# A graph network's source stage: rows landed one per descriptor, three of eight source tiles filled by accumulating gathers

## The reference, cut to what matters

```python
h = relu(layernorm(x));  x = x + attention_layer(h, edges)      # first layer
h = relu(layernorm(x))                                          # second layer:
msg = concat([h[row], h[col], edge_attr])                       # row = src, col = dst
t   = relu(msg @ W1 + b1) @ W2 + b2
x   = x + segment_sum(t, row, n)                                # sums over the SOURCE node
```

## Time and profile before

| | us |
|---|---|
| median of three runs | 5703.44 |
| the profiled execution | 5709.14 |
| its span, first to last instruction | 5707.3 |
| TensorE busy | 5097.3 (89%) |
| weight loads busy | 4028.8 (71%) |
| VectorE busy | 3955.6 (69%) |
| GpSimd busy | 3878.4 (68%) |
| ScalarE busy | 2972.5 (52%) |
| source stage, first load to last gather | 4364.8 to 5668.9 |

### The profile page before, as it was taken

One profiled execution on the slowest core, in us unless ns is written; L12 is line 12 of the kernel. 1 busy time (PEld: TensorE's weight loads), 2 busy tenths in 40 slices (PEclk: granted clock), 3 DMA queues, 4 the chain that ended last, 5 costly groups with the idle time before them and its releaser, 6 DMA issues.

```text
span 5707.3 us, 159502 instructions
## 1 busy us (share of the span) xinstructions
PE 5097.3 (89%) x33692; PEld 4028.8 (71%) x33693; DVE 3955.6 (69%) x14408; ACT 2972.5 (52%) x8485; POOL 3878.4 (68%) x3713
## 2 busy tenths in 40 slices
PE   4888888888888885999999999999997999999999
PEld 3677777767777774677666666666665787777877
DVE  6778878878887886455555555555545888888887
ACT  3566666666666653333333333333223777777776
POOL 4777777777777774677777777777776555555553
PEclk6888888898888887999999999999998999999999
DMA  4522222222222234999999899998886999999997
GB/s 109 163 53 54 52 53 54 53 53 53 53 54 53 54 105 135 268 271 268 263 261 261 255 265 264 260 260 260 258 256 191 216 221 219 215 217 218 220 218 191
DMA packets 859992, 990.85 MB, mean 174 GB/s; under 512 B 307993, under 2 KB 663225, under 8 KB 859776
## 3 DMA queue, kind: packets, MB, share of 16 engines
q1 hardware_dynamic: 662496, 608.23, 41.0%
q0 software_dynamic: 190592, 378.22, 24.7%
q10 hardware_dynamic: 6816, 3.38, 0.2%
HBM read 726.65 MB, written 262.76 MB: 173 GB/s over the span
## 4 chain that ended last, share of the span: by engine, by line
PE 56%; DMA 11%; issue 11%; POOL 9%; DVE 8%; DVEq 3%; ACT 2%; POOLq 0%; ACTq 0%; SPq 0%
PE bank L1705 12%; PE bank L1538 10%; PE bank L1628 9%; PE bank L1630 7%; PE bank L1695 7%; DMA xr<-arena 6%; POOL xr L547 5%; POOL arena L499 4%; PE bank L1464 2%; DMA arena<-h_tab,arena 2%; DVE arena L1055 2%; DVE arena L945 2%; PE bank L1618 2%; DMA arena<-p_tab,arena 1%; PE bank L1686 1%
## 5 line engine op out<-in xcount | busy, mean ns | idle before, releaser
L499 POOL DMA_INDIRECT arena<-h_tab,arena x1612 | 1564.3, 970 | 549.2 <-issue 407.6
L547 POOL DMA_INDIRECT xr<-arena x1612 | 1569.6, 974 | 515.4 <-issue 341.6
L1538 PE MATMUL bank<-arena 128*128 128x136 f32 x6448 | 1314.0, 332 | 72.7 <-DVE arena L1055 8.4
L719 ACT ACTIVATE arena<-bank 128x256 f32<-128x256 f32 x1612 | 593.5, 385 | 1393.6 <-PE bank L1630 944.5
L1628 PE MATMUL bank<-arena 128*128 128x256 f32 x3224 | 1031.4, 402 | 82.6 <-DVE arena L1251 44.1
L561 POOL DMA_INDIRECT arena<-p_tab,arena x428 | 669.7, 1565 | 630.9 <-DMA arena<-p_tab,arena 527.0
L1538 PEld LDWEIGHTS bank<-arena 128*128 128x128 f32 x6448 | 983.7, 215 | 158.1 <-DVE arena L1055 62.0
L626 ACT ACTIVATE arena<-bank 128x256 bf16<-128x256 bf16 x1612 | 613.6, 381 | 806.0 <-PE bank L1464 725.1
L1630 PE MATMUL bank<-arena 128*128 128x256 f32 x3224 | 977.1, 385 | 0.0
L1705 PE MATMUL bank<-arena 128*128 128x257 f32 x3424 | 898.5, 384 | 7.0 <-issue 4.9
L1055 DVE TENSOR_TENSOR arena<-arena,bank 128x272 f32 x1612 | 693.5, 430 | 183.5 <-PE bank L1538 152.4
(11 more groups left out here) (255 smaller groups left out, 6550.6 us busy)
## 6 DMA issues: line engine op xcount, KB each, us to landing
arena<-xr SPq DMA_DIRECT2D x428, 516.0 KB, 3.9
arena<-q_tab SPq DMA_DIRECT2D x1612, 128.0 KB
arena<-in_edge_attr SPq DMA_DIRECT2D x61, 832.0 KB
arena<-rel_tab SPq DMA_DIRECT2D x124, 224.0 KB
arena<-h_tab,arena POOLq DMA_INDIRECT x1612
xr<-arena POOLq DMA_INDIRECT x1612
arena<-rel_tab SPq DMA_DIRECT2D x124, 192.0 KB
xr<-arena SPq DMA_DIRECT2D x26, 516.0 KB
```

What stands on the lines that cost most here:

```text
L499: pool.indirect_dma_start(G[:, q, t, :], None, h_tab, bass.IndirectOffsetOnAxis(ap=idx[:, q, t:t + 1], axis=0)).then_inc(sem(f"gath{q}"), 16)
L547: pool.indirect_dma_start(xr, bass.IndirectOffsetOnAxis(ap=pos[:, q, t:t + 1], axis=0), Rb[:, t, :], None).then_inc(sem(f"scat{m}"), 16)
L1538: last = pe.matmul(PSB[3 + t % 2][:, k * H * MW:(k + 1) * H * MW], OH[:, (t + 2 * q) % 4, k * P:(k + 1) * P], flat(msg[:, t, :, :]), start ...
```

## The change

Two things are changed in the source stage and nowhere else.

First, `XR` gets a row pitch of 264 floats instead of 258 (`XP = HID + 8`), so that the two rows of a pair no longer lie in one run in a partition. A slot is loaded by two transfers, one for each pair, each of which writes 258 floats at a pitch of 264; both count up the same semaphore, and `hotp` waits for both. To make room, the tensor `OHq` moves to another region. A row then starts at a multiple of 1056 bytes in its buffer instead of 1032.

Second, `added` also holds for both pairs of the slots with odd s. Of a turn's 16 tiles 6 are gathered instead of 4: one in a slot of even s, two in a slot of odd s. Everything that asks `added` follows: an odd slot's first pair turns one tile and makes three matmuls instead of six, copies and adds half as much, and its relu waits for the slot's gathers too; `sidx` has two columns; `source_add` issues two gathers behind one wait.

```diff
+XP = HID + 8
-        XR, OHp, OHq = S([NS, CP, PR * RW]), S([SB, PR, P]), S([4, PR, P], BF16)
+        XR, OHp = S([NS, CP, PR * XP]), S([SB, PR, P])
-        sidx = S([NS, CP], I32)
+        sidx, OHq = S([NS, CP], I32), S([4, PR, P], BF16)
-        added = lambda s, k: k == 1
+        added = lambda s, k: k == 1 or s % 2 == 1
...
-                sp.dma_start(XR[:, s, :, :], xr[bass.ds(c * (CP * GR), CP * GR), :].rearrange("(k p j) w -> p k (j w)", p=P, j=PR)).then_inc(sem(f"xr_in{s}"), 16)
+                for k in range(CP):
+                    sp.dma_start(XR[:, s, k, :].rearrange("p (j w) -> p j w", j=PR)[:, :, 0:RW],
+                                 xr[bass.ds(c * (CP * GR) + k * GR, GR), :].rearrange("(p j) w -> p j w", j=PR)).then_inc(sem(f"xr_in{s}"), 16)
...
-                    pool.indirect_dma_start(XR[:, s, k, RW:RW + HID], None, p_tab,
+                    pool.indirect_dma_start(XR[:, s, k, XP:XP + HID], None, p_tab,
...
-                    dve.wait_ge(sem(f"xr_in{s}"), 16 * (i + 1))
+                    dve.wait_ge(sem(f"xr_in{s}"), 16 * CP * (i + 1))
                     n = len(NADD[s])
-                    V.tensor_scalar(sidx[:, s, CP - n:], XR[:, s, CP - n:, RW + HID + 1], 0.0, None, ALU.max).then_inc(sem("idx_ready"), 1)
+                    V.tensor_scalar(sidx[:, s, CP - n:], XR[:, s, CP - n:, XP + HID + 1], 0.0, None, ALU.max).then_inc(sem("idx_ready"), 1)
...
-                    c, direct = j * RW + HID, j and added(s, k)
+                    c, direct = j * XP + HID, j and added(s, k)
```

## The result

The changed kernel takes 5949.9 us (median of four runs, 5939.04 to 5957.36) against 5703.51 us (four runs of the kernel before): a ratio of 1.0432, interval 1.0418 to 1.0446, or 246 us more. 5953 was predicted.

The account below looks back on a forecast made before the run. TensorE (2.90 us) and the gathers' cycle both lay close to the source stage's 3.02 us slot. Paired gathers would make it 3.605: 0.585 x 428 = +250 us on 5703, giving 5953, range 5770 to 6110.

Parts of the forecast that it names:

- The 4.6 us: Source stage, odd slot: second gather's time from start to landing, taken midway between 3.85 and 5.30 us.
- pair's cycle: GpSimd, source stage: next odd slot's gathers wait until both land; two slots take 0.74 + 1.87 + 4.6 = 7.21 us.
- lower bound, 3.85 us: Second gather's shortest time to landing, from the source stage's first gather with hardly any load beside its data.
- no second bound: Source stage: the buffers' loop, 3.56 us a slot, stays just under the gathers' 3.605, without slack.
- loop of the four buffers: A load waits for the relu four slots earlier; load, gathers, two relus and 2.25 us queueing give 14.25, 3.56 a slot.
- The forecast of the chain: Source stage's chain of waits should be the gathers, with TensorE's L1705 and L1695 no longer filling it.
- 0.37 us more for the second transfer: SP's issue of a slot's second load: 0.37 us on SP and as much on the slot's landing.
- Packets: Load queue, source stage: 544 packets a slot at 60 ns, 2.06 us; with gathers' 1.26, 3.32 us a slot.
- rival B: Quiet gathers: second gather lands near 3.85 us; DMA engines' 3.32 us (+128) or gather cycle's 3.23 (+90) decides; chance 0.15.
- Rival C: Aligned rows land gathers sooner, TensorE decides: up to -81 us, 5622; chance 0.05 faster, 0.04 about unchanged.
- 2.71 us: TensorE's own work per source-stage slot after the change, down from 2.90; 75% of 3.605, so not the bound.
- The fall of the clock: TensorE, source stage: even at a granted 0.88 its work needs 3.08 us a slot, still covered by 3.605.

Follow-up runs that it names:

- after_no_loads: Changed kernel with the source stage's loads after the first turn left out, VectorE waiting for the relu four slots ago instead: 5788.3 us, ratio 1.0132.
- two_long_loads: Kernel before with two loads a slot, one a pair, both rows in one descriptor, old pitch of 258: 5744.4 us, ratio 1.0076.
- gathers_ahead: Kernel before with six gathers a turn, a semaphore per slot's gathers, two early long-row loads, `sidx` one pair earlier: 5858.9 us, ratio 1.0271.
- pitch260: Changed kernel with a row pitch of 260 floats, 1040 bytes, no multiple of 32, instead of 1056 bytes: 5959.5 us, ratio 1.0434.

## Why the prediction came out

- **Size and sign: right, the size partly by luck.** 250 us were forecast, 246 measured. The slot is 3.59 us where 3.605 was worked out. The 4.6 us was the middle of two bounds, taken because neither was nearer, and it came out at 4.5.
- **The pair's cycle: right as a cycle, term by term.** 0.74, 1.85 (1.87 forecast) and 4.62 us (4.6 forecast) in the turn shown, and 120 of 139 pairs waited as foretold. Its lower bound, 3.85 us for the second gather alone, was measured as 3.78 in a turn of after_no_loads, 3.81 in the mean.
- **That it alone decides: wrong.** The step "no second bound" is the one that failed. The prediction put a loop of the four buffers, with the gathers in it, 0.04 us below the pair's cycle. The loop that the chain shows goes through VectorE's order, has no gather in it and closes after two slots, at 3.54 us a slot; that the two figures lie so near is luck. The forecast of the chain, gathers instead of TensorE, failed with it: the chain shows TensorE and loads. And a third cycle, the distance from `sidx` to the relu in the written order, was not in the prediction at all; with the wait by parity taken away it left 3.66 us. So the pair's cycle is one of three of nearly the same length, and which of them sets a given slot of the changed kernel was not separated further.
- **The loads: undersized.** By the prediction's own terms for the loop (0.37 us more for the second transfer) a slot of the old single gather would take (3.9 + 0.37 + 5.30 + 0.63 + 2.25)/4 = 3.11 us. That two_long_loads takes 3.12 confirms little, as the 2.25 us is only what closed the sum of the loop before, and TensorE makes up most of that kernel's chain. With single rows it is 3.33. The price missing was that of the split: SP's issue of 256 short descriptors, 0.543 us, was taken as the 0.373 of 256 long ones, and it counts twice in a lap. On the changed kernel's chain the load takes 0.55 us, 0.19 between the two issues, and 4.58 in the mean (43 loads), where the prediction had 0.37 and 3.9.
- **Packets: near.** 151428/279 = 543 packets a slot (544 forecast), 55 ns each (60 forecast), so 1.88 us of the loads' queue against 2.06. The gathers' queue is 37.3%, 1.34 us a slot against 1.26. Full DMA engines (rival B's 3.32 us) were not the limit of the changed kernel: its packets take 1.88 + 1.34 = 3.22 us of 3.59, and gathers_ahead moves the same bytes (in long rows) in 3.37 us a slot.
- **Rival C fell.** An aligned target neither shortens the landing beside loads (pitch260) nor, by much, alone (3.78 us against the 3.85 of the stage's start with the old pitch). The Trainium skill (Collectives: The Full Stack, Rules for kernel authors) has the rule, written for the buffers of collectives, that 32-byte alignment prevents a read-modify-write. For this indirect add these runs show no price of it: 4.52 us to the landing without the alignment and 4.51 with it.
- **TensorE.** Its 2.71 us never decided. Its share in the stage is 82% and not 75%, 2.96 us of 3.59. In gathers_ahead, with the same matmuls at a granted 1.00, it is 92% of 3.37, or 3.1 us, so the busy time, with its modelled ends, is no measure of TensorE's own work here. The fall of the clock that the prediction covered for didn't come: 0.99 granted in the stage.

## What to carry to other kernels

Where engines take work in a fixed order, each asynchronous step has several cycles through it: the buffer it refills, the counter that it is numbered by, and the distance in the program between its start and its first reader. A wait in the written order also holds up the older work behind it, which can close a loop sooner than the ring of buffers does. Before moving work onto such a step, work out each of them, not only the tightest today: here the second and third lay close behind, and easing one gained nothing. And a transfer inside such a loop costs its issue time, which here grew with the split into short descriptors, even on an engine that "only waits".

## What the runs showed of the hardware that was not expected

- SP's issue time did not go with the bytes: 333 ns for 128 runs of 2064 bytes, 373 ns for 256 of them, 543 ns for 256 runs of 1032 bytes, which are the bytes of the first.
- TensorE had 0.99 of full clock in the changed source stage at 82% busy, and 0.88 in a stretch of the first stage at 84%: between these two the busy share doesn't tell the granted clock.
- Gathers with an add issued behind each other by GpSimd at 1.85 us intervals land 3.8 us after their start with no loads beside them (after_no_loads), and 4.5 us in the mean beside loads in single rows (the changed kernel); a second gather in a row added its interval of 1.85 us, not a second landing.
